# Asking for the first two experts' lists, weights and rows before the attention stage has ended

## The chip, the cores and the metric

The kernel runs on one core of a Trainium2 chip. The metric is the device time of one execution in microseconds (us): all input loads, the whole computation and the stores of the result.

## The reference, cut to what matters

One decoder layer over 64 sequences of 128 tokens, 256 wide: a linear-recurrence mixer, cross attention, and a mixture of experts, each with a residual and a layer norm. The change lies where the second turns into the third.

```python
x = _layernorm(x + mixer(x))
x = _layernorm(x + cross_attention(x, ctx))       # these rows are called x2 below
# mixture of experts: 32 experts, 4 of them for each token, at most 1280 tokens for one expert
shared = silu(xf @ sg) * (xf @ su) @ sd
top_scores, top_idx = top_k(masked_scores, 4)
buf[e_s, p_s] = xf[tok]                            # rows gathered by expert
h = silu(buf @ wg) * (buf @ wu)                    # per expert, 256 -> 512
out_e = h @ wd                                     # per expert, 512 -> 256
x = _layernorm(x + shared + routed)
```

## The kernel before, in words

Four stages follow one another, each a block of five instruction streams (SP, PE, ACT, DVE, POOL) with a barrier of all engines between two blocks: mixer, attention, experts, combination. All DMAs but the indirect ones are issued by SP, the indirect ones by POOL.

**Attention.** 16 groups of 4 sequences. All rows stand in one buffer `x` of 16 slots (`rows(k.x, g)`, 4 KB in each partition per group), which is released when the stage ends. As each group is done, SP stores its rows to `x_rows` in HBM, and POOL scatters, with 16 indirect DMAs a group, a list entry (token, destination, gate) for each token and chosen expert into `slot_token`. After the last group comes a tail: the routing of the last two groups, DVE's list of work items (`plan.count_items`, `plan.list_items`), and between them on PE, ACT and DVE the shared expert for the first three groups (`shared_turn`, `shared_up`, `shared_down`, `shared_sum`). SP's tail is `store(NG - 1)`, `store_shared(0)`, `plan.deliver` (the item list goes through HBM into `k.plan`, where engines can read it into registers), `store_shared(1)` and `(2)`, and the waits for all that was stored. POOL's tail ends with the last scatter.

**Experts.** An item is 256 list slots of one expert; there are 92 in this run. For each, SP reads the item's expert and first slot into registers and loads the list piece (`e_tok`, 3 KB), and gate, up and down weights (`e_raw_g`, `e_raw_u`, `e_raw_d`, 512 KB each); POOL gathers the rows (`e_xg`, two indirect DMAs of 128 rows); PE transposes them; ACT and DVE split weights and rows into a high and a low part; PE runs gate, up and down products out of three matmuls per chunk; POOL scatters the result. All of this is double-buffered. The first two items are unrolled: SP's `first` (L1777) issues list, gate and up of item 0, the same of item 1, both down loads, and two loads of x2 rows for the combination. ACT's `first` splits the four weight pieces of item 0 before it takes the transposed rows, and DVE follows it:

```python
                def first():
                    for m in range(HC):
                        weights_high(0, 0, 0, m)
                    turned(0)
                    item(0, 0, 0)
```

PE starts with `turn(0, 0, 0)`, which waits for the gathered rows, and `up(0, 0)`, which waits for the low parts of rows and weights. Each engine adds 1 or 16 to its semaphores on entry (`begin`) and reads the number of items into a register (`items_of`).

**Combination.** It adds shared rows, x2 rows and the four expert outputs of each token in a ring of four buffers (`acc`, `res`, `part`), and runs the shared expert for the other 13 groups.

## Time and profile before

| what | us |
|---|---|
| median of 3 runs | 2105.52 |
| lowest and highest | 2104.67, 2109.74 |
| span of the profiled execution | 2166.1 |
| attention stage ends, expert stage starts, in the profiled execution | between 1014.8 and 1020.6 |

The profile is one execution of its own, 60.6 us longer than the median; no other time of it is given than its span. Positions below are microseconds from the start of that span. PE is the matmul engine, PEld its weight loads, SPq the queue of DMAs that SP issues. In a timeline row the first number is the start, the second the time until the last of the merged instructions is done, and the brackets say how long the engine sat idle before and what ended it.

### The profile page before, as it was taken

Reading aid. Unit: us, or ns where it says so; the run is one execution under the profiler, and the core shown is the slowest. Engines: PE = TensorE matmul, PEld = TensorE weight load, DVE = VectorE, ACT = ScalarE, POOL = GpSimd, SP = SyncE. Lnnn points to the kernel's source line nnn. Section 1 sums busy time; section 2 is a strip of 40 time slices with the busy share of each in tenths; the row PEclk is TensorE's granted clock in tenths of the full one; section 3 lists DMA queues with packets and bytes.
Section 4 is the critical chain, followed back from the end, with each engine's and each line's share of the span. In section 5 each row is a group of like instructions: output and inputs, shape, how many; then the busy total and the mean of one; then the engine's idle time right before and its main releaser. Section 6 shows DMA issues by size and latency. Waiting matters only on the chain. (4 is left out here: it accounts for less than half of the span.)

```text
span 2166.1 us, 51696 instructions
## 1 busy us (share of the span) xinstructions
PE 2001.3 (92%) x14320; PEld 1794.5 (83%) x14320; DVE 1521.7 (70%) x3647; ACT 1254.7 (58%) x3478; POOL 1493.7 (69%) x1695
## 2 busy tenths in 40 slices
PE   8999799999999999875899999999999999579998
PEld 6888587777777777664899999999999999558887
DVE  7888467777776777662677777888888888335554
ACT  4556465655664556531677777777777777324443
POOL 5565315766665666663688888888888888458765
PEclk9999899999999999987899999999999999789999
DMA  4300132242233222401677766776777677356542
GB/s 140 88 0 1 43 127 79 85 151 78 78 105 113 94 78 93 131 20 53 230 229 235 232 234 226 230 240 229 236 235 236 232 238 233 122 216 237 203 165 98
DMA packets 244909, 329.95 MB, mean 152 GB/s; under 512 B 50074, under 2 KB 167234, under 8 KB 244836
## 3 DMA queue, kind: packets, MB, share of 16 engines
q1 hardware_dynamic: 218788, 279.97, 40.0%
q0 software_dynamic: 26048, 49.10, 6.2%
q8 instruction: 35, 0.57, 0.1%
q14 instruction: 38, 0.31, 0.0%
HBM read 236.17 MB, written 77.18 MB: 145 GB/s over the span
## 5 line engine op out<-in xcount | busy, mean ns | idle before, releaser
L1345 POOL DMA_INDIRECT slot_token<-a_entry,a_slot_i x256 | 261.8, 1022 | 158.2 <-issue 70.3
L1827 POOL DMA_INDIRECT part_rows<-e_out,e_dest x184 | 228.3, 1241 | 71.0 <-issue 56.6
L1819 POOL DMA_INDIRECT e_xg<-x_rows,e_tok x188 | 207.0, 1101 | 93.9 <-issue 56.2
L1960 ACT ACTIVATE e_sg<-e_g 128x256 f32<-128x256 f32 x368 | 141.8, 385 | 196.0 <-PE e_g L1652 186.5
L2009 DVE TENSOR_TENSOR e_h<-e_sg,e_u 128x256 f32<-128x256 f32 x368 | 157.3, 428 | 65.4 <-PE e_u L1652 28.2
L1170 ACT ACTIVATE a_prob<-a_s,a_ntop 128x128 f32<-128x128 f32 x512 | 180.9, 402 | 4.9 <-DVE a_ntop L1524 4.9
L2024 DVE TENSOR_SCALAR e_out<-e_d,e_dest 128x256 f32<-128x256 f32 x184 | 80.6, 480 | 139.6 <-PE e_d L1652 138.8
L1835 POOL TENSOR_TENSOR e_wd1l<-e_raw_d,e_wd1h 128x256 fp32r<-128x256 f32 x184 | 145.4, 827 | 5.7 <-ACT e_wd1h L1940 4.8
L1835 POOL TENSOR_TENSOR e_wd0l<-e_raw_d,e_wd0h 128x256 fp32r<-128x256 f32 x184 | 145.9, 829 | 4.8 <-ACT e_wd0h L1940 3.8
L1032 PE MATMUL a_o<-a_wo,a_ot 128*128 128x256 f32 x512 | 125.2, 389 | 8.4 <-DVE a_ot L1591 8.3
L1652 PE MATMUL e_d<-e_wd1h,e_ht1h 128*128 128x256 f32 x368 | 108.5, 295 | 24.5 <-issue 24.5
L1524 DVE TENSOR_REDUCE a_ntop<-a_s 128x4 f32<-128x512 f32 x128 | 82.4, 686 | 64.5 <-remote 41.6
L1170 ACT ACTIVATION_READ_ACCUMULATOR a_prob<-a_s,a_ntop 128x1 f32 x512 | 124.1, 242 | 0.0
L1032 PEld LDWEIGHTS a_o<-a_wo,a_ot 128*128 128x128 f32 x512 | 95.0, 196 | 20.0 <-DVE a_ot L1591 9.2
L2267 ACT ACTIVATE f_sg<-f_g 128x512 f32<-128x512 f32 x52 | 31.1, 599 | 134.4 <-PE f_g L1652 134.4
L1652 PE MATMUL e_g<-e_xth,e_wg1h 128*128 128x256 f32 x368 | 104.3, 284 | 3.9 <-DVE e_xtl L1995 3.7
L1652 PE MATMUL e_d<-e_wd0h,e_ht0h 128*128 128x256 f32 x368 | 107.6, 292 | 0.0
L1652 PE MATMUL e_g<-e_xth,e_wg0h 128*128 128x256 f32 x368 | 105.1, 286 | 1.4 <-DVE e_xtl L1995 1.4
L1652 PE MATMUL e_d<-e_wd1h,e_ht1l 128*128 128x256 f32 x368 | 104.5, 284 | 0.0
L1652 PE MATMUL e_d<-e_wd1l,e_ht1h 128*128 128x256 f32 x368 | 104.5, 284 | 0.0
L1652 PE MATMUL e_g<-e_xtl,e_wg0h 128*128 128x256 f32 x368 | 104.2, 283 | 0.0
L1652 PE MATMUL e_u<-e_xth,e_wu0l 128*128 128x256 f32 x368 | 104.2, 283 | 0.0
(397 smaller groups left out, 7604.8 us busy)
## 6 DMA issues: line engine op xcount, KB each, us to landing
e_raw_g<-in_eg SPq DMA_DIRECT2D x94, 512.0 KB
e_raw_u<-in_eu SPq DMA_DIRECT2D x94, 512.0 KB
e_raw_d<-in_ed SPq DMA_DIRECT2D x93, 512.0 KB
part_rows<-a_zero SPq DMA_DIRECT2D x16, 2048.0 KB
f_part<-part_rows SPq DMA_DIRECT2D x16, 2048.0 KB, 9.5
x<-in_x SPq DMA_DIRECT2D x16, 512.0 KB, 4.0
x_rows<-x SPq DMA_DIRECT2D x16, 512.0 KB
out_rows<-f_res SPq DMA_DIRECT2D x16, 512.0 KB, 10.1
```

Of the source, the lines that this page charges most:

```text
L1032: last = pe.matmul(bank_o[:, 0:D], ot[:, m, :], wo[:, m, :], start=(m == 0), stop=(m == IC - 1))
L1170: last = act.activation(prob[b % 2][:, h, :], bank_s[r][:, m * T:(m + 1) * T], ACT.Exp, bias=ntop[b % 2][:, h:h + 1], accum_out=den[b % 2] ...
L1345: pool.indirect_dma_start(k.slot_tok, bass.IndirectOffsetOnAxis(ap=slot_i[:, j, q:q + 1], axis=0), entry[:, j, q, :], None, bounds_check=S ...
L1524: last = dve.tensor_reduce(ntop[b % 2][:, r * IC:(r + 1) * IC], bank_s[r][:].rearrange("p (m t) -> p m t", m=IC), AX.X, ALU.max, negate=True)
L1652: last = pe.matmul(out, a, b, start=(n == 0 and t == 0), stop=(n == len(chunks) - 1 and t == 2))
L1819: pool.indirect_dma_start(xg[a][:, n, :], None, k.x2_d, bass.IndirectOffsetOnAxis(ap=tok[a][:, n, 0:1], axis=0))\
L1827: pool.indirect_dma_start(k.part_d, bass.IndirectOffsetOnAxis(ap=dest[a][:, n, 1:2], axis=0), out[a][:, n, :], None).then_inc(put[a], 16)
L1835: pool.tensor_tensor(wd[par][1][:, m, :], raw_d[par][:, m, :], wd[par][0][:, m, :].bitcast(F32), ALU.subtract).then_inc(dl_rdy, 1)
L1960: act.activation(sg[m % 2][:], bank_g[m % 2][:, 0:SETW], ACT.Silu).then_inc(sg_rdy, 1)
L2009: dve.tensor_tensor(hid[m % 2], sg[m % 2][:], bank_u[m % 2][:, 0:SETW], ALU.mult)\
L2024: dve.tensor_scalar(out[a][:, n, :], bank_d[0:RT, (n % 2) * D:(n % 2 + 1) * D], gate[:, n, 2:3], None, ALU.mult).then_inc(out_rdy, 1)
L2267: act.activation(sg[m % 2][:], bank_g[m % 2][:], ACT.Silu).then_inc(sg_rdy, 1)
```

## The change

Gate, up and down weights, list pieces and gathered rows of items 0 and 1 are asked for inside the attention stage. Their SBUF buffers are no longer allocated by the expert stage: they become views of slots 3 to 9 of `x`, which is now kept for the whole kernel, and whose slots 3 to 9 hold rows that have been stored to HBM. The combination's `acc`, `res` and `part` (16 slots in all) become views of `x` as well. Two list buffers and ten semaphores are made for the whole kernel. The zero fill of `x_rows`' spare rows gets a semaphore of its own (`spare_in`), so that POOL can wait for it.

```diff
                 store(NG - 1)
                 store_shared(0)
                 plan.deliver(sp)
+                sp.wait_ge(x2_out, DMA + 16 * NG)
+                for w in range(2):
+                    e = expert_of(sp, k, w)
+                    sp.dma_start(k.raw_g[w], one_expert(k.gate_d, e)).then_inc(k.g_in[w], 16)
+                    sp.dma_start(k.raw_u[w], one_expert(k.up_d, e)).then_inc(k.u_in[w], 16)
+                    start = slots_of(sp, k, w)
+                    if w == 0:
+                        sp.wait_ge(scattered, 16 * TG * K * NG)
+                        apart(sp, k.past_sp)
+                    sp.dma_start(k.tok[w][:], k.slot_tok[bass.ds(start, SETW), :].rearrange("(p n) a -> p n a", n=TI))\
+                        .then_inc(k.tok_in[w], 16)
+                for w in range(2):
+                    e = expert_of(sp, k, w)
+                    sp.dma_start(k.raw_d[w], one_expert(k.down_d, e)).then_inc(k.d_in[w], 16)
                 for n in range(1, SG):
                     store_shared(n)
-                sp.wait_ge(x2_out, DMA + 16 * NG)
-                sp.wait_ge(filled, DMA + 16 * (NG + 1 + SG))
+                sp.wait_ge(spare_in, 16)
+                sp.wait_ge(filled, DMA + 16 * (NG + SG))
                 sp.wait_ge(blanked, DMA + 32)
...
                 scatter(NG - 1, range(TG), False)
+                pool.wait_ge(x2_out, DMA + 16 * NG)
+                pool.wait_ge(spare_in, 16)
+                for w in range(2):
+                    pool.wait_ge(k.tok_in[w], 16)
+                    apart(pool, k.past_pool)
+                    gather_rows(pool, k, w)
...
                 def first():
-                    for w in range(2):
-                        load_tok(w, w)
-                        load_gate(w, w)
-                        load_up(w, w)
-                    for w in range(2):
-                        load_down(w, w)
                     for i in range(2):
                         first_rows = k.x2_d[(SG + i) * GW:(SG + i + 1) * GW, :]
...
                 def first():
-                    gather(0, 0, 0)
-                    gather(1, 1, 0)
                     item(0, 0, 0)
                     item(1, 1, 0)
...
-        acc, res = ([p.sb(f"{n}{i}", [P, TG, D]) for i in range(RING)] for n in ("acc", "res"))
-        part = [p.sb(f"part{i}", [P, TG, K, D]) for i in range(2)]
+        acc, res = ([grouped(in_rows(k, n * RING + i)) for i in range(RING)] for n in range(2))
+        part = [k.x[:, (2 * RING + K * i) * GX:(2 * RING + K * (i + 1)) * GX]
+                .rearrange("p (t q d) -> p t q d", t=TG, q=K) for i in range(2)]
...
+def in_rows(k, g):
+    return k.x[:, g * GX:(g + 1) * GX]
...
+def first_tiles(k, sem):
+    def wide(g):
+        return in_rows(k, g).rearrange("p (c n) -> p c n", c=DC)
+    k.raw_g, k.raw_u = [wide(SG + i) for i in range(2)], [wide(SG + 2 + i) for i in range(2)]
+    k.raw_d = [in_rows(k, SG + 4 + i).rearrange("p (c n) -> p c n", c=HC) for i in range(2)]
+    k.xg = [in_rows(k, SG + 6)[:, i * TI * D:(i + 1) * TI * D].rearrange("p (n d) -> p n d", n=TI) for i in range(2)]
...
+def gather_rows(pool, k, a):
+    for n in range(TI):
+        pool.indirect_dma_start(k.xg[a][:, n, :], None, k.x2_d,
+                                bass.IndirectOffsetOnAxis(ap=k.tok[a][:, n, 0:1], axis=0)).then_inc(k.rows_in[a], 16)
```

`expert_of` and `slots_of` read the expert and the first slot of an item from `k.plan` into a register, as the expert stage did.

## Rows read from the trace of the kernel before

**Rows 1.** The page's head: span and number of instructions.
```profile
span 2166.1 us, 51696 instructions
```

**Rows 2.** Windows: stretch, its us, busy us of each engine, granted clock, DMA.
```profile
core 0: us, PE busy (x) PEld busy (x) DVE busy (x) ACT busy (x) POOL busy (x), PEclk, DMA share, GB/s
...
996.00:1000.00 4.00, 3.34 (x8) 2.70 (x9) 1.98 (x3) 2.10 (x4) 0.54 (x2) 0.50 0.01 2
1000.00:1004.00 4.00, 4.00 (x18) 2.97 (x16) 1.29 (x2) 1.86 (x4) 0.00 (x0) 0.97 0.01 2
...
1030.00:1036.00 6.00, 4.59 (x21) 4.19 (x20) 1.65 (x3) 1.50 (x3) 1.05 (x2) 0.50 1.06 355
1036.00:1039.00 3.00, 3.00 (x20) 3.00 (x20) 1.42 (x4) 1.75 (x5) 0.00 (x0) 0.70 1.09 361
1200.00:1800.00 600.00, 600.00 (x5071) 599.92 (x5070) 481.28 (x1000) 435.99 (x1133) 524.83 (x533) 1.00 0.71 232
```

**Rows 3.** Timeline of all engines, from the tail's last PE work to expert work.
```profile
1013.43 0.28 PE L1652 MATMUL a_o<-wd_both,a_htl 128*128 128x256 f32 x1
...
1023.07 1.07 POOL L1819 DMA_INDIRECT e_xg<-x_rows,e_tok  x1 [25.86 <-DMA e_tok<-slot_token]
...
1025.07 1.15 ACT L1933 ACTIVATE e_wg0h<-e_raw_g 128x512 fp32r<-128x512 f32 x2 [19.57 <-DMA e_raw_g<-in_eg]
...
1027.90 1.15 ACT L1933 ACTIVATE e_wu0h<-e_raw_u 128x512 fp32r<-128x512 f32 x2 [1.68 <-DMA e_raw_u<-in_eu]
1028.56 1.29 DVE L1989 TENSOR_TENSOR e_wu0l<-e_raw_u,e_wu0h 128x512 fp32r<-128x512 f32 x2 [1.53 <-ACT e_wu0h L1933]
1028.88 1.21 POOL L1819 DMA_INDIRECT e_xg<-x_rows,e_tok  x1 [3.47 <-DMA e_tok<-slot_token]
...
1029.47 1.12 PE L1873 MATMUL e_t<-ident,e_xg 128*128 128x128 f32 x4 [15.76 <-DMA e_xg<-x_rows,e_tok]
...
1030.62 0.60 ACT L1946 ACTIVATE e_xth<-e_t 128x512 fp32r<-128x512 f32 x1 [1.57 <-PE e_t L1873]
...
1031.25 0.69 DVE L1995 TENSOR_TENSOR e_xtl<-e_t,e_xth 128x512 fp32r<-128x512 f32 x1 [1.40 <-ACT e_xth L1946]
...
1032.00 0.58 PE L1652 MATMUL e_g<-e_xth,e_wg0h 128*128 128x256 f32 x1 [1.41 <-DVE e_xtl L1995]
```

**Rows 4.** Timeline of SP's DMA queue, 980 to 1040 us (21.59 spans both stores).
```profile
984.11 0.25 SPq L724 DMA_DIRECT2D plan<-item_list  x1
993.26 21.59 SPq L933 DMA_DIRECT2D shared_rows<-x  x2
1020.60 0.36 SPq L1739 DMA_DIRECT2D e_tok<-slot_token  x1
1021.72 0.38 SPq L1746 DMA_DIRECT2D e_raw_g<-in_eg  x1
...
1024.00 0.35 SPq L1739 DMA_DIRECT2D e_tok<-slot_token  x1
```

**Rows 5.** Waits of SP's queue, 980 to 1030 us: total us, times, longest.
```profile
SPq L947 <- DMA shared_rows<-x: 2.5, 1, 2.5
```

**Rows 6.** Timelines at the two other changes of stage: engine starts.
```profile
236.15 2.06 ACT L369 ACTIVATE x<-x,m_off,m_rs 128x256 f32<-128x256 f32 x4
...
239.60 1.94 PE L963 MATMUL a_a<-ident,x 128*128 128x128 f32 x8 [3.98 <-issue]
...
1905.47 0.38 SPq L2114 DMA_DIRECT2D xs<-shared_rows  x1
```

**Rows 7.** Timeline of PE at the start of the combination stage.
```profile
1905.83 1.94 PE L2197 MATMUL f_t<-ident,xs 128*128 128x128 f32 x8 [10.55 <-DVEq L72]
```

**Rows 8.** Timeline of the attention tail, 990 to 1000 us, three engines.
```profile
992.48 0.69 DVE L1571 TENSOR_TENSOR x<-a_o,x 128x512 f32<-128x512 f32 x1 [9.87 <-remote]
...
996.01 1.08 ACT L1224 ACTIVATE v<-a_s 128x512 f32<-128x512 f32 x2 [19.61 <-remote]
996.61 0.60 POOL L1353 TENSOR_SCALAR a_entry<-a_entry 128x16 int32<-128x16 int32 x2 [2.83 <-DMA slot_token<-a_entry,a_slot_i]
```

**Rows 9.** Timeline of PE near the end of the expert stage.
```profile
1890.28 0.57 PE L1652 MATMUL e_d<-e_wd1h,e_ht1h 128*128 128x256 f32 x1 [24.53 <-issue]
```

More of the change, by code:

```diff
@@ L900, in _ @@
                 sp.wait_ge(zero_rdy, 1)
-                sp.dma_start(k.x2_d[B * T:B * T + SETW, :].rearrange("(p n) d -> p n d", n=TI), spare).then_inc(filled, 16)
+                sp.dma_start(k.x2_d[B * T:B * T + SETW, :].rearrange("(p n) d -> p n d", n=TI), spare).then_inc(spare_in, 16)
                 def store(g):
@@ L1662, in expert_stage @@
         p = Parts(nc, ctx, "e_")
[L1663 to L1664 removed]
+        raw_g, raw_u, raw_d, tok, xg = k.raw_g, k.raw_u, k.raw_d, k.tok, k.xg
         wg = [[p.sb(f"wg{i}{h}", [P, DC, HID], F32R) for h in "hl"] for i in range(2)]
         wu = [[p.sb(f"wu{i}{h}", [P, DC, HID], F32R) for h in "hl"] for i in range(2)]
[L1667 removed]
         wd = [[p.sb(f"wd{i}{h}", [P, HC, D], F32R) for h in "hl"] for i in range(2)]
[L1669 removed]
         dest = [p.sb(f"dest{i}", [RT, TI, 3], I32) for i in range(2)]
[L1671 removed]
         xt = [p.sb(f"xt{h}", [P, DC, SETW], F32R) for h in "hl"]
@@ L1680, in expert_stage @@
         hid = [bank[:, 0:SETW] for bank in bank_h]
-        g_in, u_in, d_in, tok_in, x_in, dest_in = ([p.sem(f"{n}{i}") for i in range(2)]
-                                                   for n in ("g_in", "u_in", "d_in", "tok_in", "x_in", "dest_in"))
+        g_in, u_in, d_in, tok_in, x_in = k.g_in, k.u_in, k.d_in, k.tok_in, k.rows_in
+        dest_in = [p.sem(f"dest_in{i}") for i in range(2)]
         put = [p.sem(f"put{i}") for i in range(2)]
@@ L1723, in _ @@
                 begin(sp, dma=(*g_in, *u_in, *d_in, *tok_in, *dest_in, *k.xs_in[:2]))
-                def one(d, e):
-                    return d[:, bass.ds(e, 1), :, :].rearrange("p a c n -> p (a c) n")
-                def expert(w):
-                    return sp.value_load(k.plan[0:1, bass.ds(w * 4 + 1, 1)], min_val=0, max_val=E - 1)
-                def slots(w):
-                    return sp.value_load(k.plan[0:1, bass.ds(w * 4, 1)], min_val=0, max_val=SLOTS)
                 def load_tok(w, a):
-                    start = slots(w)
+                    start = slots_of(sp, k, w)
                     if at_least(w, 2):
@@ L1817, in gather @@
                     apart(pool, k.past_pool)
-                    for n in range(TI):
-                        pool.indirect_dma_start(xg[a][:, n, :], None, k.x2_d,
-                                                bass.IndirectOffsetOnAxis(ap=tok[a][:, n, 0:1], axis=0))\
-                            .then_inc(x_in[a], 16)
+                    gather_rows(pool, k, a)
                 def put_rows(w, a):
@@ L2349, with one_expert, expert_of, slots_of @@
     pass
+def in_rows(k, g):
[6 more added lines that the diff above has]
+    k.xg = [in_rows(k, SG + 6)[:, i * TI * D:(i + 1) * TI * D].rearrange("p (n d) -> p n d", n=TI) for i in range(2)]
+    k.g_in, k.u_in, k.d_in, k.tok_in, k.rows_in = ([sem(f"{n}{i}") for i in range(2)]
+                                                   for n in ("g_in", "u_in", "d_in", "tok_in", "rows_in"))
+    k.gate_d = k.weights["eg"].rearrange("e (c p) n -> p e c n", p=P)
+    k.up_d = k.weights["eu"].rearrange("e (c p) n -> p e c n", p=P)
+    k.down_d = k.weights["ed"].rearrange("e (c p) n -> p e c n", p=P)
+def one_expert(weights, e):
+    return weights[:, bass.ds(e, 1), :, :].rearrange("p a c n -> p (a c) n")
+def expert_of(sp, k, w):
+    return sp.value_load(k.plan[0:1, bass.ds(w * 4 + 1, 1)], min_val=0, max_val=E - 1)
+def slots_of(sp, k, w):
+    return sp.value_load(k.plan[0:1, bass.ds(w * 4, 1)], min_val=0, max_val=SLOTS)
+def gather_rows(pool, k, a):
+    for n in range(TI):
+        pool.indirect_dma_start(k.xg[a][:, n, :], None, k.x2_d,
+                                bass.IndirectOffsetOnAxis(ap=k.tok[a][:, n, 0:1], axis=0)).then_inc(k.rows_in[a], 16)
 def build(nc, dram):
@@ L2374, in build @@
         k.shared_d = nc.dram_tensor("shared_rows", [SG * GW, D], F32).ap()
+        k.tok = [sb(f"tok{i}", [RT, TI, 3], I32) for i in range(2)]
+        k.x, k.weights = sb("x", [P, B * D]), dram
+        first_tiles(k, lambda name: ctx.enter_context(nc.semaphore(name)))
         with ExitStack() as early:
```

25 lines of the change are left out of this document (8 added, 17 removed).

## The prediction

> **What bounds the kernel now.** I read the page's head first: the profiled execution spans 2166.1 us [rows 1], 60.6 us more than the median of the runs. Part of that excess is visible as pauses in which an engine waits for nothing the kernel asks for (24.53 us on PE in one item [rows 9], 9.87 us on DVE in the attention tail [rows 8]). So I make the sum of the change on the profiled positions, and say separately what such a pause covers.
>
> Then the windows. In the long middle of the expert stage PE is busy for 600.00 of 600 us at full clock, with the DMA engines at a share of 0.71 [rows 2]. So this stage is bound by PE: a microsecond saved before PE's first product moves every item, and the combination behind them, forward by the same. A microsecond saved on loads alone, once PE runs, is worth nothing.
>
> Then the timeline between the stages, which is where the change acts. The reader should follow the chain by hand. PE's last matmul of the attention tail starts at 1013.43 [rows 3]; DVE adds it, SP issues the last shared-row store, whose issue ends at 993.26 + 21.59 = 1014.85 [rows 4], and then waits 2.5 us for its landing [rows 5], so the stage is over at about 1017.4. SP's first load of the expert stage comes at 1020.60 [rows 4]. ACT starts at 1025.07, when the first gate weights are there, and again at 1027.90 for the up weights; PE's transposes start at 1029.47, when the gathered rows are there; the first product starts at 1032.00 [rows 3]. Between 1013.7 and 1032.0 PE does four transposes. Its long wait, 15.76 us, ends on the gather; the gather in its turn waited for the list [rows 3]. This is what the change addresses: list 2.47 us from issue to use (1020.60 to 1023.07), gather 6.4 us from POOL's start to PE's.
>
> **The change part by part.** *The start of the expert stage.* With lists, weights and rows on the chip, ACT, DVE and PE start as soon as the barrier lets them. Call ACT's first instruction S. For S the trace has three indications. SP's first issue at 1020.60 [rows 4] follows two register reads (number of items, first slot), where ACT has only one; two SP loads with one read each lie 1.12 us apart, of which 0.36 is the issue, so a read is about 0.75 us, and S = 1020.60 - 0.75 = 1019.9. As the early bound I take the first change of stage: ACT's last work ends at 236.15 + 2.06 = 238.21 and PE starts at 239.60, 1.4 us later [rows 6], which gives 1017.4 + 1.4 = 1018.8. As the late bound, in the combination stage, whose first rows are already on the chip, PE starts 0.36 us after SP's first issue (1905.83 against 1905.47) [rows 6, 7], which gives 1021.0. I take 1019.9.
>
> From S the chain is ACT's four pieces, 1.15 us for each two, so the second pair starts at S + 1.1; DVE ends the second pair 1.95 us after that pair began (1028.56 + 1.29 - 1027.90), at S + 3.05; meanwhile PE has transposed (1.12) and ACT has split the rows (0.60); DVE takes the rows' low part after the weights', and PE's first product starts 0.75 us behind its beginning (1032.00 - 1031.25): S + 3.8 [rows 3]. With S = 1019.9 that is 1023.7 instead of 1032.0: **8.3 us less**, and 9.4 to 7.2 by the two bounds. Nothing behind it eats this: from here on item 0 needs the down weights, item 1 its weights and rows, all of them on the chip. Item 2's loads wait for what DVE and PE have done with item 0, so they move forward with it.
>
> *The clock.* Before, PE ran at 0.50 of its clock up to 1036 and at 0.70 on average from 1036 to 1039 [rows 2], so the first product saw about 6.6 us of the lower level (1.2 GHz), after an idle stretch of 15.8 us. After the shorter pause in the tail [rows 8] PE was busy for 3.34 us at 0.50 from 996 to 1000, and the stretch from 1000 to 1004 has 0.97 [rows 2]: 3 to 4 us. The new idle stretch, 6 us to the transposes and 10 to the products, lies between. If the low level ends as early as after the short gap, half of the 3 us difference is won, 1.5 us; if nothing changes, none. I take **0.5 us less**.
>
> *SP's queue in the tail.* SP moves eight loads behind the delivery of the plan, and in front of two shared-row stores. The plan is asked for at 984.11 [rows 4], so gate and up of item 0 go out near 987. Then SP waits for all scatters, which POOL sees landed at 996.61 [rows 8]. That is the new wait: behind it stand list 0, gate 1, up 1, list 1, down 0, down 1 and both shared-row stores. With 0.4 us for each issue and 0.75 for each of four reads, some 5.5 us, SP is through at about 1002.2. The store of group 1 was issued at 993.26 before [rows 4], but nobody waits for it before the stage ends. The store of group 2 is ready only at about 1014.5, 0.36 us before its issue ends at 1014.85, and is issued then, as before. The four weights behind the wait are 2.1 MB; at 355 GB/s [rows 2] that is 5.9 us, and they have landed by 1006. So on the profiled positions the cost is zero, covered by PE, ACT and DVE's work on the shared expert, with some 8 us to spare.
>
> That cover contains the 9.87 us pause. If the timed runs do not have it, the last store is ready at 1004.6. It then stands behind the rest of the weights (to 1006) and the group 1 store (0.52 MB, 1.5 us), and four gathers (0.52 MB, 1.5 us) mix in: it lands up to 4.4 us later. If they do have it, nothing. I take **1.5 us more**, and 0 and 4.4 as ends.
>
> The row to weigh here is DMA share and rate in this part of the tail: 0.01 and 2 GB/s from 996 to 1004 [rows 2], so there is room for the loads. The Trainium skill (DMA: Bandwidth & Descriptors, "Issuing engines are not separate DMA queues") says that transfers started by SP and by POOL run on the same 16 engines and interleave. By that rule weights, scatters and stores share one rate, which is the 4.4 us end; by queues of their own the gathers' 1.5 us would fall away.
>
> *POOL.* It moves four gathers ahead of the barrier and gains waits for rows, spare rows and lists; nothing is queued behind them in this stage but the barrier. List 0 is there 2.5 us after its issue near 997, and two gathers take 2.6 us. List 1 took 4.9 us behind two weight loads (1024.00 to 1028.88) [rows 3, 4] and is asked for near 999.5, so the last gather is issued by 1007. The barrier opens at 1017.4, or 1007.5 without the pause: cost zero either way, but then by only half a microsecond.
>
> *Memory.* The views are of the same shape and use the same instructions, and the x2 rows of slots 3 to 9 were stored long before; no instruction is added in the expert or combination stage. Cost zero.
>
> **The sum.** -8.3 - 0.5 + 1.5 = -7.3 us. On the profiled positions, with the pause, it is -8.8: span 2157.3. The items behind are bound by PE in both, so I carry -7.3 over to the median: 2105.5 - 7.3 = **2098.2 us**.
>
> **Rivals.** *A, the gain is partly given back:* either the tail's store lands at the late end (4.4) or another wait takes the place of the loads, such as ACT, DVE or PE starting 2 to 4 us after S because three streams enter code that they used to enter under cover of the loads. For it speaks that all of them sat idle until 1025 or later, so the trace shows nothing of what they could have done earlier; against it, the starts at the other changes of stage, 1.4 us and 0.36 us [rows 6, 7]. With both bounds, 7.2 - 4.4 = 2.8 us of gain: 2102.7.
>
> *B, the clock and the barrier go well:* S by its early bound, 1.5 us from the clock, no loss in the tail: 9.4 + 1.5 = 10.9 us, 2094.6.
>
> *C, slower:* SP's wait for the scatters holds the last store. Weights of item 0 now run while the last few scatters are issued. If each scatter, 12-byte entries in 128 pieces, had to stand behind such loads, the wait at 996.61 would end later by d, and SP is through at 1002.2 + d. It decides from d = 12.3 us on the profiled positions, or 2.4 us without the pause; beyond that each microsecond is paid in full. The change is slower than before from 8.8 us beyond that point on, and by over 0.3% from 15.1 us beyond it, 17.5 us in all. 1 MB of weights at 355 GB/s lasts 3 us, which speaks strongly against it. At 17.5 us: 2112.
>
> *D, it does nothing:* something else sets PE's first product, for instance the rows of item 0 landing after the barrier anyway. They are asked for 16 us before 1017.4, or 6 us without the pause, and took 6.4 us at worst in the trace. Time: 2105.5.
>
> **How the numbers follow.** Measurement of this kernel can tell about 0.3%, 6.3 us: faster means below 2099.2. Forecast (gain 6.3 to 9.5): 0.50. B: 0.12. A: 0.28. D: 0.05. C and its kind: 0.05. So faster 0.62, same 0.33, slower 0.05. The range reaches from B, 2094.6, to past A, 2104.0; it leaves out D, C and the far end of B.
>
> **What would show it.** In the profile after: e_raw_g, e_raw_u, e_raw_d and e_tok of two items in SP's queue between 987 and 1003, with a hole up to the scatters' landing; POOL's four gathers before 1008; ACT's first split within 1 us of 1019.9, counted as 2.5 us behind the landing of the last store; the first product 3.8 us later; PE's share of 1.00 from the third item on. The prediction is wrong if ACT starts more than 2 us after that, if the last store's landing moves away from DVE's last sum, or if PE's work on the first items grows new waits for loads.

## The result, and the profile after

| kernel | median of the runs, us | lowest and highest | ratio to before, 95% interval |
|---|---|---|---|
| before | 2105.1 | 2104.17, 2109.74 | |
| changed | 2094.2 | 2092.2, 2095.48 | 0.9943 [0.9928, 0.9957] |
| changed, a second series on another chip | 2096.8 | 2095.08, 2098.51 | 0.9960 [0.9947, 0.9972] |

Faster, as forecast, but by 10.9 us in the first series where 7.3 were forecast: 0.4 us beyond the fast end of the range. The second series gives 8.3 us. The spans are 1.7 to 1.8 us below the times of the same executions.

The profiled execution shown ahead of the prediction was 60.6 us too long. The kernel before was therefore profiled once more (e1 below: time 2108.6, span 2106.8), and the comparisons here are with that trace.

The changed kernel's timeline at the change of stage, all engines; the brackets give the idle time before the instruction and what ended it. They answer to [rows 3, 4]:

```profile
939.76 0.41 SPq L946 DMA_DIRECT2D x<-in_eg  x1
940.27 0.41 SPq L947 DMA_DIRECT2D x<-in_eu  x1
947.64 0.36 SPq L952 DMA_DIRECT2D tok<-slot_token  x1
...
950.28 1.07 POOL L2380 DMA_INDIRECT x<-x_rows,tok  x1 [2.12 <-DMA tok<-slot_token]
...
951.93 1.55 SPq L956 DMA_DIRECT2D x<-in_ed  x2
953.52 4.54 SPq L933 DMA_DIRECT2D shared_rows<-x  x2
...
956.95 0.69 DVE L1591 TENSOR_TENSOR x<-a_o,x 128x512 f32<-128x512 f32 x1 [2.11 <-PE a_o L1672]
957.05 0.96 POOL L2380 DMA_INDIRECT x<-x_rows,tok  x1 [4.43 <-DMA tok<-slot_token]
958.31 0.96 POOL L2380 DMA_INDIRECT x<-x_rows,tok  x1 [0.30 <-issue]
965.74 1.15 ACT L1925 ACTIVATE e_wg0h<-x 128x512 fp32r<-128x512 f32 x2 [17.01 <-issue]
...
966.16 1.11 PE L1865 MATMUL e_t<-ident,x 128*128 128x128 f32 x4 [9.24 <-issue]
...
969.55 0.58 PE L1672 MATMUL e_g<-e_xth,e_wg0h 128*128 128x256 f32 x1 [2.29 <-DVE e_xtl L1987]
```

And SP's waits in the same execution (line, what it waited for, total us, times, longest), which answer to [rows 5]:

```profile
SPq L62 <- DMA slot_token<-a_entry,a_slot_i: 6.1, 1, 6.1
SPq L961 <- DMA shared_rows<-x: 4.6, 1, 4.6
```

The same place in the kernel before (e1), one row for each link of its chain:

```profile
958.60 0.69 DVE L1571 TENSOR_TENSOR x<-a_o,x 128x512 f32<-128x512 f32 x1 [2.06 <-PE a_o L1652]
959.32 0.37 SPq L933 DMA_DIRECT2D shared_rows<-x  x1
965.43 0.36 SPq L1739 DMA_DIRECT2D e_tok<-slot_token  x1
...
969.83 1.15 ACT L1933 ACTIVATE e_wg0h<-e_raw_g 128x512 fp32r<-128x512 f32 x2 [19.36 <-DMA e_raw_g<-in_eg]
...
974.52 1.11 PE L1873 MATMUL e_t<-ident,e_xg 128*128 128x128 f32 x4 [15.96 <-DMA e_xg<-x_rows,e_tok]
...
977.04 0.58 PE L1652 MATMUL e_g<-e_xth,e_wg0h 128*128 128x256 f32 x1 [1.41 <-DVE e_xtl L1995]
```

From DVE's last sum of the attention to PE's first product it was 977.04 - 958.60 = 18.4 us and is 969.55 - 956.95 = 12.6 us: **5.8 us** won at the head. PE's transposes no longer end their wait on the gather; the bracket says "issue", which here covers the barrier between the stages. That is the change doing what it says. Two things went against it. The last store takes 4.6 us to land, where it took 2.5 [rows 5]. And the barrier waits for POOL. At the end of the attention block (L877) each engine's queue of instructions ends with a DRAIN, and the barrier's first event comes when the last DRAIN has ended. The changed kernel's, and behind them those of e7, whose gathers are back in the expert stage (count, then ns, then the start in us):

```profile
L877 POOLq EVENT_SEMAPHORE  x2: 17/17/17, 964.4 to 964.5; - x2
...
L877 POOLq DRAIN  x1: 7047/7047/7047, 957.3 to 957.3; - x1
...
L877 SPq DRAIN  x1: 13/13/13, 962.9 to 962.9; - x1
```

```profile
L877 POOLq EVENT_SEMAPHORE  x2: 17/17/17, 961.7 to 961.7; - x2
L877 POOLq DRAIN  x1: 4097/4097/4097, 947.4 to 947.4; - x1
...
L877 SPq DRAIN  x1: 13/13/13, 961.6 to 961.6; - x1
```

In the changed kernel SP is done at 962.9, and POOL's DRAIN ends only at 957.3 + 7.05 = 964.4: the barrier opens 1.5 us later than the last store asks for. By the packets of the trace the last gathered rows land at 962.57, 1.8 us before that DRAIN ends. In e7, with no gathers in the tail, POOL has long been done when SP comes. So the barrier, too, opens later than before: 3.9 us behind DVE's last sum in e1, 7.5 us here. Of these 3.6 us more, 2.1 are the store and 1.5 the gathers. From the barrier to the first product it was 14.5 us and is 5.1. The difference of the two is the 5.8 us.

From the first product to the first transposes of the combination (PE `f_t`) it was 1846.77 - 977.04 = 869.7 us and is 1834.52 - 969.55 = 865.0: **4.8 us** more, inside a stage of which the prediction said that only the clock would change, by 0.5. The other 3.1 us between the two spans (2106.8 and 2093.1) lie ahead of DVE's last sum (1.6) and behind `f_t` (1.5); the same two stretches differ by as much between executions of kernels with the same memory, so nothing is read from them. The windows show where the 4.8 us come from. PE's busy time, its count of matmuls (x), and the granted clock (PEclk); first e1:

```profile
core 0: us, PE busy (x) PEld busy (x) DVE busy (x) ACT busy (x) POOL busy (x), PEclk, DMA share, GB/s
1000.00:1200.00 200.00, 200.00 (x1694) 200.00 (x1693) 154.36 (x334) 145.24 (x380) 150.05 (x178) 1.00 0.70 233
1500.00:1700.00 200.00, 200.00 (x1694) 199.99 (x1693) 163.44 (x334) 145.04 (x379) 175.46 (x179) 1.00 0.72 235
```

and the changed kernel:

```profile
1000.00:1200.00 200.00, 200.00 (x1732) 200.00 (x1731) 157.25 (x343) 149.22 (x389) 174.70 (x182) 1.00 0.72 239
1500.00:1700.00 200.00, 199.14 (x1689) 197.05 (x1688) 168.31 (x333) 145.15 (x378) 175.68 (x178) 1.00 0.71 232
```

In the first window PE is busy for 200.00 of 200 us at a clock of 1.00 in both, and yet does 1732 matmuls instead of 1694. "100% busy" had hidden a rate. In the second the gain is gone: 1689, PE has 0.86 us of idle time, and PEld 2.95. Item by item (from one group of transposes to the next) the changed kernel takes 8.78 us on average from the third item to the 31st, near 1240 us, and 9.02 after it; the kernel before takes 8.98 and 8.99. Counted from the first product, the changed kernel leads by 0.5 us at the second item, by 6.0 at the 34th, and by 4.3 at the start of the last: the faster items give about 5.5 us and the slower ones take 1.7 back. So some 4 us net come from the rate of the items and 0.5 from the clock.

### The profile page after: what moved, and what is told of

It reads as the page before. It is cut to its first block and busy times, and to the rows that moved or that the text cites. A ratio compares the mean times of both kernels' runs of the same rounds, so it can differ in the third digit from the quotient of the medians.

```text
span 2093.1 us, 51690 instructions
## 1 busy us (share of the span) xinstructions
PE 1973.9 (94%) x14320; PEld 1772.8 (85%) x14320; DVE 1533.5 (73%) x3647; ACT 1255.7 (60%) x3478; POOL 1488.2 (71%) x1695
## 5 line engine op out<-in xcount | busy, mean ns | idle before, releaser
L2380 POOL DMA_INDIRECT x<-x_rows,tok x188 | 206.8, 1100 | 75.9 <-issue 56.1
L1829 POOL TENSOR_TENSOR e_wd1l<-x,e_wd1h 128x256 fp32r<-128x256 f32 x184 | 145.5, 828 | 5.7 <-ACT e_wd1h L1932 4.8
L1829 POOL TENSOR_TENSOR e_wd0l<-x,e_wd0h 128x256 fp32r<-128x256 f32 x184 | 145.5, 829 | 5.4 <-ACT e_wd0h L1932 4.4
L1672 PE MATMUL e_d<-e_wd1h,e_ht1h 128*128 128x256 f32 x368 | 107.0, 291 | 24.5 <-issue 24.5
L1046 PEld LDWEIGHTS a_o<-a_wo,a_ot 128*128 128x128 f32 x512 | 93.8, 193 | 19.2 <-DVE a_ot L1611 8.8
L1672 PE MATMUL e_g<-e_xth,e_wg0l 128*128 128x256 f32 x368 | 103.1, 280 | 0.0
## 6 DMA issues: line engine op xcount, KB each, us to landing
out_rows<-x SPq DMA_DIRECT2D x16, 512.0 KB, 10.3
```

Of the source, the lines that this page charges most:

```text
L1046: last = pe.matmul(bank_o[:, 0:D], ot[:, m, :], wo[:, m, :], start=(m == 0), stop=(m == IC - 1))
L1672: last = pe.matmul(out, a, b, start=(n == 0 and t == 0), stop=(n == len(chunks) - 1 and t == 2))
L1829: pool.tensor_tensor(wd[par][1][:, m, :], raw_d[par][:, m, :], wd[par][0][:, m, :].bitcast(F32), ALU.subtract).then_inc(dl_rdy, 1)
L2380: pool.indirect_dma_start(k.xg[a][:, n, :], None, k.x2_d, bass.IndirectOffsetOnAxis(ap=k.tok[a][:, n, 0:1], axis=0)).then_inc(k.rows_in[a] ...
```

## The experiments

Each kernel was timed against the kernel before on the same chip. The attention's tail alone, from DVE's sum near 841 us to its last, differs between executions of all these kernels from 111 to 116 us, old ones and new ones alike, a spread as wide as that of the medians; so the lengths inside a trace carry the argument, and the medians confirm it. Several medians lie 1 to 5 us below the time expected (e4, e5, e11, e16, e17), and those of e2 and e3 2 us above it. The changed kernel was not timed beside e2 to e4; its own ratio to the kernel before, 0.9943 or 0.9960 (e8), is what theirs are held against.

The head differs between executions as well, by the tail. This table has every kernel with loads in the tail, and e1 (us; all but the landing counted from DVE's last sum, the first column back from it):

| kernel | down loads all issued, before the last sum | last store lands in | SP comes to the barrier | barrier opens | first product |
|---|---|---|---|---|---|
| changed | 3.5 | 4.6 | 5.9 | 7.5 | 12.6 |
| e8, the same | 3.7 | 4.3 | 5.7 | 7.2 | 12.3 |
| e3 | 1.2 | 6.3 | 7.7 | 8.7 | 13.9 |
| e6 | 1.1 | 6.5 | 7.8 | 8.8 | 13.9 |
| e2 | -0.1 | 8.1 | 9.6 | 10.6 | 15.8 |
| e7, no gathers in the tail | 1.3 | 5.3 | 6.7 | 6.7 | 16.9 |
| e4, no down loads in the tail | | 3.1 | 4.5 | 6.5 | 11.6 |
| e12, the same | | 2.6 | 3.9 | 6.4 | 11.6 |
| e1 | | 2.5 | 3.9 | 3.9 | 18.4 |

The closer the down loads come to the last store, the longer it takes to land; without them it takes 2.6 to 3.1 us. With gathers in the tail the barrier opens 1.0 to 2.5 us behind SP, and in every kernel without them 0.02 to 0.03 us behind it. From the barrier to the first product all seven kernels with early loads and gathers take 5.13 us. So the 5.8 us of the head are those of one execution: with the same loads in the tail the others give 6.1 (e8), 4.6 (e3), 4.5 (e6) and 2.7 (e2).

**e1, the kernel before again** (no edit).

> The kernel before, profiled once more, to have a trace without the pauses that made its first one 60 us longer. Theory POOL (the expert stage is paced by POOL's instructions, not by PE's): from the third item on POOL runs without idle time but for the fixed gaps between its indirect DMAs, items come every 8.9 to 9.0 us, and the change gained where POOL's unbroken chain starts earlier, by about 9 to 12 us counted from DVE's last sum of the attention stage. Theory PE (the one of the prediction): the start of PE's first product moved by the whole gain, so counted from DVE's last sum the first product comes some 11 us later here than in the changed kernel, not 5.6 us as the two traces at hand say.

2108.55 us in its one execution. The trace is the one used above. Neither theory came out as written: the first product came 5.8 us later than in the changed kernel and not 11, and in the first window POOL is busy for 150 of 200 us and waits for ACT. The idle stretch of 9.87 us in the tail [rows 8] is not in it. The 24.5 us before the last `e_d` group [rows 9] are, in both kernels, whose spans are free of any excess:

```profile
1831.65 0.58 PE L1652 MATMUL e_d<-e_wd1h,e_ht1h 128*128 128x256 f32 x1 [24.53 <-issue]
```

So this row was read wrongly: it is a fixed part of the stage's end (24.5 or 24.6 us in every kernel here), presumably PE's way through the rounds of the loop that have no items, and no part of the 60.6 us. Those lie in the attention stage, which from PE's first instruction to DVE's last sum took 774.2 us in the first profile and 715.2 in this one.

**e2, 5 us more work for POOL**, once, behind items 0 and 1 of the changed kernel:

```diff
+                    for n in range(2):
+                        pool.tensor_tensor(in_rows(k, 13 + n), in_rows(k, 11), in_rows(k, 12), ALU.add)
```

> The changed kernel with two additions of 128 x 1024 elements on POOL, into unused slots of x, right after its work for item 1: 4.8 us more on POOL, by the 2.40 us of the same shape in the combination stage. Nothing waits for them but POOL itself. Theory POOL: 4 to 5 us slower than the changed kernel, 2098 to 2099, because POOL has no idle time behind that point. Theory PE: within 1 us of the changed kernel, because POOL has slack in every item.

2101.0 us, ratio 0.9978 [0.9966, 0.9990]. The addition took 5.21 us, and the stage from first product to `f_t` was 869.9 us long instead of 865.0: nearly all of it was paid, within the first ten items. POOL has no slack over the stage of the changed kernel. The time is 2 us above what was expected; the late landing of this execution (8.1 us, in the table) has nothing to do with the edit, which stands behind the barrier.

**e3, POOL's four subtractions of an item in one instruction** (changed kernel; the two waits on them adapted):

```diff
-                    for m in range(HC):
-                        pool.wait_ge(dh_rdy, ONE + HC * w + m + 1)
-                        pool.tensor_tensor(wd[par][1][:, m, :], raw_d[par][:, m, :], wd[par][0][:, m, :].bitcast(F32),
-                                           ALU.subtract).then_inc(dl_rdy, 1)
+                    pool.wait_ge(dh_rdy, ONE + HC * (w + 1))
+                    pool.tensor_tensor(wd[par][1][:], raw_d[par], wd[par][0][:].bitcast(F32),
+                                       ALU.subtract).then_inc(dl_rdy, 1)
```

> The changed kernel with POOL's four subtractions of 128 x 256 per item (2.81 us) made as one of 128 x 1024 (2.40 us). Same result. Theory POOL: an item gets 0.4 us shorter until PE's own 8.62 us bind, so 15 to 30 us less in all, 2064 to 2079. Theory PE: no change, or up to 2 us slower, since PE's down product can start only when all four parts are done.

2081.4 us, ratio 0.9888 [0.9868, 0.9908]. The windows of e3:

```profile
1000.00:1200.00 200.00, 200.00 (x1733) 200.00 (x1732) 163.24 (x343) 149.24 (x389) 157.27 (x116) 1.00 0.73 241
1500.00:1700.00 200.00, 200.00 (x1736) 200.00 (x1736) 164.27 (x343) 149.74 (x390) 157.28 (x115) 1.00 0.73 239
```

Now the rate of the first window lasts: 8.78 us an item to the end. POOL's groups from 1500 to 1700 us, the changed kernel first (busy us, mean ns | idle before, and what ended it), show what the edit relieved:

```profile
L1821 POOL DMA_INDIRECT part_rows<-e_out,e_dest x44 | 53.3, 1211 | 10.4 <-issue 10.0 <-DMA tok<-slot_token 0.3
...
L1829 POOL TENSOR_TENSOR e_wd0l<-x,e_wd0h 128x256 fp32r<-128x256 f32 x46 | 38.7, 876 | 0.3
```

```profile
L1828 POOL TENSOR_TENSOR e_wd1l<-x,e_wd1h 128x1024 fp32r<-128x1024 f32 x12 | 28.9, 2407 | 9.4 <-ACT e_wd1h L1931 9.4
```

Four subtractions of 876 ns are 3.50 us; the one takes 2.41. In the changed kernel POOL is idle for 0.3 and 0.2 us in all ahead of its two groups of subtractions in that stretch; in e3 it waits 0.8 us an item for ACT. The gain is less than the 15 to 30 us expected, because 8.62 us is only the shorter of two kinds of item: they come at 8.62 or about 8.90, and PE's own average is 8.78. The stage is 850.8 us long, 14.2 less than in the changed kernel.

**e4, the two loads of down weights left in the expert stage** (changed kernel):

```diff
-                for w in range(2):
-                    e = expert_of(sp, k, w)
-                    sp.dma_start(k.raw_d[w], one_expert(k.down_d, e)).then_inc(k.d_in[w], 16)
                 for n in range(1, SG):
                     store_shared(n)
...
                 def first():
+                    load_down(0, 0)
+                    load_down(1, 1)
```

> The changed kernel with the two down loads left at the start of the expert stage (1 MB less in the attention tail). It prices the contention in the tail: in the changed kernel the last shared-row store took 4.6 us to land, against 2.5 us before. Both theories: the landing comes back to 2.5 to 3 us. If the down weights are not missed later, the kernel gains 1 to 2 us (2092 to 2093); if their arrival near 971 delays the list load for item 2 and with it POOL, it gains nothing or loses up to 2 us.

2089.4 us, ratio 0.9922 [0.9905, 0.9939], on a chip on which the changed kernel itself was not timed. In the trace the last store lands in 3.1 us instead of 4.6, and from last sum to first product it is 11.6 us instead of 12.6, the stage behind it 865.8: 1 us, not 5. SP comes to the barrier 1.5 us earlier, but POOL's DRAIN now holds it for 2.0 us more. e12 below does not show the 5 us either.

The kernels from here on, but for e7, e8, e11 and e12, ask where the faster matmuls come from.

**e5, the changed kernel's memory with the old order of loads:** lists, weights and gathers of both items are asked for in the expert stage again, in the tiles of the changed kernel.

> This kernel has the changed kernel's tiles in the changed kernel's places, but the first two items' lists, weights and rows are all asked for in the expert stage again, as before. Theory L (TensorE's matmul spacing depends on where the tiles lie): within the expert stage the 48 gate and up products of an item take 5.4 to 5.6 us instead of 5.70, so the time from the first transposes of the expert stage to the first ones of the last stage is 2 to 4 us shorter than the 872.25 us of the kernel before (868.36 in the changed one), and the time is about 2101 to 2103. Theory O (the spacing changed with the order, that is with how the engines' work falls against one another after an earlier start): 5.70 us and 872 us as before, the time 2105, a ratio of 1.000. Theory B (the page of the kernel before had only an unlucky execution): no difference in spacing between any of the kernels beyond what repeats differ by.

2099.6 us, ratio 0.9969 [0.9958, 0.9979]. From last sum to first product 19.2 us (18.2 to 19.0 in the kernels with the old memory); from there to `f_t` 866.0 us, as in the changed kernel, and 1729 matmuls in the first window. So the 4 us of the stage come with the memory, and not with the earlier start.

**e6, the two lists 64 bytes wide instead of 24** (changed kernel):

```diff
-        k.tok = [sb(f"tok{i}", [RT, TI, 3], I32) for i in range(2)]
+        k.tok = [sb(f"tok{i}", [RT, TI, 8], I32)[:, :, 0:3] for i in range(2)]
```

> The changed kernel with each of the two lists in 64 bytes per partition instead of 24, so that all later tiles lie 80 bytes further on; nothing else. Theory L in its narrow form (the offset of the tiles within a block of memory decides): the item pitch differs from the changed kernel's, to 8.98 us throughout with 5.70 us for gate and up (time about 2097 to 2098), or faster throughout. If the offset is of no account: as the changed kernel, 2093 to 2096, gate and up 5.44 to 5.6 us.

2097.4 us, 0.9961 [0.9948, 0.9974]; the stage 863.8 us. Items of 8.75 and 9.00 us: still the faster rate. So moving all later tiles on by 80 bytes does not bring the old one back.

**e7, only the gathers back in the expert stage** (changed kernel).

> The changed kernel with only the four indirect gathers of the first two items moved back to the expert stage; lists and weights are still asked for in the attention's tail. The prediction's own sum: the gathers cannot begin before the barrier is passed, so GpSimd's two gathers of the first item and the landing of their rows are on the path again: the first transposes move from the last sum + 9.2 us to about + 13 to 14 us, the time is 4 to 5 us above the changed kernel's, 2098 to 2100. Rival (the gathers were not what held the start, the weights' landing was): within 1.5 us of the changed kernel.

2099.1 us, 0.9968 [0.9956, 0.9981]. From last sum to first product 16.9 us: 4.3 to 4.5 us over the changed kernel's 12.6 and 12.3, as expected. That is a difference of two effects. From the barrier to the first product it is 10.2 us instead of 5.1, and the barrier opens 0.5 to 0.8 us earlier, because no gathers hold it. The medians differ by 2.3 (e8).

**e8, the changed kernel again,** beside e5 to e7.

> The changed kernel again, on the chip that runs the three beside it: 2093 to 2096; gate and up of an item 5.44 us in some items and 5.6 on average. Theory B (the spacing differs from execution to execution) expects another pattern: 5.70 throughout, or 5.44 throughout.

2096.8 us, 0.9960 [0.9947, 0.9972]. 12.3 us at the head and 865.4 in the stage: the pattern repeats.

**e9 and e10, the old tiles in another order or higher.** e9 allocates raw weights and gathered rows behind all other tiles; e10 puts 36 KB of nothing ahead of all:

```diff
+        p.sb("pad", [P, 36 * 256])
         raw_g = [p.sb(f"raw_g{i}", [P, DC, HID]) for i in range(2)]
```

> The kernel before with one difference: the tiles that the transfers of the expert stage fill (the raw gate, up and down weights and the gathered rows) are allocated behind all other tiles of that stage instead of ahead of and between them, so that the tiles TensorE reads lie 16 to 24 KB further down. Theory S (what counts is that the tiles which transfers and the other engines read are apart from those TensorE reads, as the stored rows' memory is in the changed kernel): matmul spacing of the changed kernel, 0.113 to 0.118 us, items of 8.62 and 8.90 us, the expert stage 3.5 to 4 us shorter, time 2101. Theory P (the place of TensorE's own tiles counts, high in memory in the changed kernel): no gain, as the kernel before, 8.98 us an item, 2105.

> The kernel before with an unused tile of 36 KB per partition ahead of the tiles of the expert stage: all of them lie 36 KB higher, in the same order. Theory P: spacing and items as in the changed kernel (8.62 and 8.90 us), time about 2101. Theory S: as the kernel before, 8.98 us an item, 2105. If both kernels of this pair show the changed kernel's spacing, neither S nor P but only some particular conflict of the old places is left; if neither does, the place of the tiles is not shown to be the cause.

2106.7 us, 1.0004 [0.9996, 1.0013], and 2105.3, 0.9996 [0.9987, 1.0005]. Items of 8.98 and 9.00 us. Neither brings the faster rate, so both theories as they stood fall: height alone does not do it, nor does taking the raw tiles away from between the others. But e10's height did something: its stage is 872.8 us long against e1's 869.7, and its down products start 0.1236 us apart on average instead of 0.1222.

**e11, e3's edit on the kernel before.**

> The kernel before with GpSimd's four subtractions of an item as one, the edit that made the changed kernel 13 us faster. Theory: in the kernel before TensorE sets the item at 8.98 us by its own spacing, and GpSimd only follows; relieving it gives nothing: 2104 to 2106, items 8.98 us. Rival (GpSimd set the item in both kernels): faster by 8 to 13 us here too, items 8.6 to 8.9 us.

2102.6 us, 0.9990 [0.9981, 0.9999]. Items of 8.98 us, and the windows of e11 have the old count:

```profile
1000.00:1200.00 200.00, 200.00 (x1694) 200.00 (x1693) 155.54 (x336) 145.51 (x380) 158.58 (x113) 1.00 0.71 233
1500.00:1700.00 200.00, 200.00 (x1694) 200.00 (x1693) 155.10 (x334) 144.82 (x377) 159.03 (x112) 1.00 0.71 232
```

The same edit is worth 13 us in the changed kernel and 2.5, at the limit of what can be told, in the old one, whose stage stays at 869.7 us. There PE's own rate sets the item; in the changed kernel it is POOL from about item 31 on. The old kernel was close to it: in e1's second window POOL is busy for 175.46 us and idle for 24.8, all but 0.4 of them the gaps marked "issue" ahead of its indirect instructions.

**e12, both edits,** e3's and e4's, on the changed kernel.

> The changed kernel with both edits that made it faster: GpSimd's four subtractions of an item as one, and the two loads of the down weights left in the expert stage. The first gives 13 us; of the second, 1.5 us are the landing of the tail's last store (4.6 to 3.1 us), which is all it can give if its measured 5 us were mostly scatter of runs: 2079 to 2081; if the 5 us are real and add up: 2075 to 2077.

2080.3 us, 0.9889 [0.9875, 0.9904]: e3's gain and no more by the medians, so most of e4's 5 us was scatter; a microsecond or two either way can't be told by them. Head 11.6 us, stage 851.6. It beats both kernels, the old one by 24 to 25 us.

**e13 to e15, semaphores or tiles.** e13: only the ten semaphores of the first loads are taken early, in the kernel before. e14: e5 with these semaphores back in their old place. e15: e5 with the gathered rows in tiles of their own.

> The kernel before with one difference: the ten semaphores of the first loads (weights, lists, gathered rows) are taken at the program's start, as in the changed kernel, so that all semaphores taken after them have other numbers; every tile stays where it was. Theory M (the place of the loaded tiles in the kept memory makes TensorE's spacing shorter and GpSimd's indirect transfers longer): nothing, 2105, items 8.98 us, matmuls 282 ns in the mean, an indirect instruction 0.97 to 1.00 us. Theory N (it is the numbers of the semaphores or another difference of the programs): 278 ns, items 8.62 to 8.92, indirect instructions 1.16 to 1.25 us, time 2101.

> The kernel with the changed kernel's memory and the old order of loads, with the ten semaphores back among those of the expert stage: the tiles alone are changed. Theory M: as the kernel with the changed memory and both (ratio 0.997, items 8.62 to 8.92 us, matmul 278 ns, indirect 1.16 to 1.25 us). Theory N: as the kernel before, 8.98 us and 2105.

> The kernel with the changed kernel's memory and the old order of loads, with only the two tiles of gathered rows in memory of their own again, between the down weights and the transposed rows as before. If the place of the gathered rows, which TensorE reads in its transposes and the indirect transfers fill, is what counts: items of 8.98 us, indirect instructions of 0.97 to 1.00 us. If it is the raw weights' place: 8.62 to 8.92 us and 1.16 to 1.25 us, ratio 0.997.

| | ratio, 95% interval | stage, us |
|---|---|---|
| e13 | 1.0001 [0.9987, 1.0015] | 870.1 |
| e14 | 0.9973 [0.9957, 0.9989] | 867.0 |
| e15 | 0.9987 [0.9975, 0.9998] | 867.0 |

By items (8.79 in e14 and 8.80 in e15 up to the 26th, 8.98 in e13) the tiles do it, without the semaphores and without the gathered rows. e15's median alone would hardly tell it from the kernel before. POOL's longer indirect instructions, which the expectations tied to the memory, are not tied to it: e11, with the old memory, has 1.20 and 1.17 us for them too.

**e16 to e18, which tiles.** e16: the kernel before, with raw weights, rows and lists ahead of all tiles that PE reads. e17: the same with 36 KB between them. e18: e5 with the raw weights and the gathered rows 12 KB lower.

```diff
         raw_u = [p.sb(f"raw_u{i}", [P, DC, HID]) for i in range(2)]
+        raw_d = [p.sb(f"raw_d{i}", [P, HC, D]) for i in range(2)]
+        xg = [p.sb(f"xg{i}", [RT, TI, D]) for i in range(2)]
+        tok = [p.sb(f"tok{i}", [RT, TI, 3], I32) for i in range(2)]
+        p.sb("pad", [P, 36 * 256])     # e17 only
         wg = [[p.sb(f"wg{i}{h}", [P, DC, HID], F32R) for h in "hl"] for i in range(2)]
```

> The kernel before with the tiles that transfers fill (raw weights, gathered rows, lists) all ahead of the tiles TensorE reads, no pad: TensorE's weight tiles lie 12 KB higher than before and next to one another, as in the changed kernel, but 36 KB lower than there. Theory T (TensorE's tiles next to one another without a raw tile between them, the raw ones below them): items of 8.62 to 8.92 us, 2101. Theory P2 (their absolute place, as with the 36 KB): as before, 8.98 us, 2105. Theory R (the place of the raw weights in the stored rows' memory): as before, 2105.

> The same with an unused tile of 36 KB between the raw tiles and those that TensorE reads: every tile that TensorE reads in its products then has exactly the changed kernel's place, while the raw tiles lie 24 KB lower than there. Theories T and P2: items of 8.62 to 8.92 us, 2101. Theory R: 8.98 us, 2105.

> The kernel with the changed kernel's memory and the old order of loads, with the raw weights and gathered rows 12 KB lower within the stored rows' memory; everything else in its place. Theories T and P2: as that kernel, ratio 0.997, items of 8.62 to 8.92 us. Theory R in its narrow form (a particular distance of 12 KB matters): another spacing.

2099.6 us, 0.9974 [0.9962, 0.9987]; 2095.5, 0.9949 [0.9932, 0.9965]; 2100.8, 0.9976 [0.9966, 0.9985]. Stage 862.0, 866.0 and 866.4 us. All three have the faster rate, 8.77 to 8.79 us an item up to the 26th. e16 is the kernel before with three lines moved up. Its groups of products from 1000 to 1240 us, behind those of e9, which has the same tiles in yet another order; e9 first, then e16:

```profile
L1652 PE MATMUL e_g<-e_xtl,e_wg1h 128*128 128x256 f32 x105 | 29.6, 282 | 0.0
...
L1652 PE MATMUL e_d<-e_wd1h,e_ht1l 128*128 128x256 f32 x112 | 31.5, 281 | 0.0
```

```profile
L1652 PE MATMUL e_g<-e_xtl,e_wg1h 128*128 128x256 f32 x112 | 31.1, 278 | 0.0
...
L1652 PE MATMUL e_d<-e_wd1h,e_ht1l 128*128 128x256 f32 x112 | 31.1, 277 | 0.0
```

The single matmul is listed with 281 to 282 ns in most groups of the one and 277 to 278 in most of the other, and all groups of `e_g`, `e_u` and `e_d` went down, but for `e_g<-e_xth,e_wg0h`, which has 282 in both. The spacing of their starts tells the same: in items of 8.98 us the 48 gate and up products take 5.70 us and the 24 down products 2.93; in the kernels with the faster rate 5.44 or 5.70, by the item, and in most items 2.83.

The attention's tail shows the same of other products. The shared expert's products of 512 columns start 0.227 us apart in every kernel that has `x` in its old place (e1, e9 to e11, e13, e16, e17) and 0.233, in e6 0.232, in all those with `x` in the new one. There the changed memory is the slower one, by 0.3 us over the last two groups.

**What stays open.** Shown: with the same instructions, semaphores and order of loads, the place of the tiles in SBUF alone changes the matmuls' spacing (e14, e16, against e1, e13). Excluded as what decides: the gathered rows' place (e15), 12 KB in the raw weights' place (e18), 36 KB in height (e10 has no gain by it, e16 has the gain without it), 80 bytes in the place of all tiles from the weights on (e6). One thing separates all runs without an exception: in those with the faster rate (the changed kernel, e2 to e8, e12, e14 to e18) the two lists, 24 or 64 bytes per partition each, lie ahead of the weight tiles that PE reads; in the others (before, e1, e9, e10, e11, e13) they lie behind them. Of the other tiles only the two `e_dest`, behind the weights in every kernel, are not a multiple of 1 KB, so the lists' place sets the offset between the weights and the transposed rows, which go into the same products; it sets the weights' own offset within a KB as well, and the runs do not part the two. But no kernel moved the lists alone, so this is what the runs agree with, and not a cause that was shown. A kernel that does only that would settle it; it wasn't tried.

## Why the prediction was right or wrong

**The chain at the start: right, and sized too low.** It said that ACT, DVE and PE start from the barrier and that the first product follows ACT's first split by 3.8 us; it was 969.55 - 965.74 = 3.8. ACT's first split came 1.3 us behind the opening of the barrier, which is the early bound (1.4 us) and not the 1019.9 that was taken. By that bound the chain gives 9.4 us, and it gave 9.4: 14.5 us from barrier to first product in e1, 5.1 in the changed kernel.

**The tail: sized too low, and one wait in it missed.** The term was 1.5 us, with 4.4 as its end; the barrier opened 3.6 us later (3.9 to 7.5 behind the last sum), and 6.7 in e2. One of the prediction's own signs of being wrong, the last store's landing moving away from DVE's last sum, was there. Of the 3.6 us, 2.1 are the store behind the weights, the mechanism that the prediction named. The other 1.5 are the gathers: "The barrier opens at 1017.4, or 1007.5 without the pause: cost zero either way" counted when the last gather is issued, and the barrier waits for POOL's DRAIN, which ends 1.8 us behind the rows' landing. List 1 held that gather until 958.31. So the head gave 9.4 - 3.6 = 5.8 us where 8.3 - 1.5 = 6.8 were expected, two misses that partly cancel; that the total is so near is luck.

The rule weighed in the tail (the Trainium skill, DMA: Bandwidth & Descriptors, "Issuing engines are not separate DMA queues") has transfers started by SP and by POOL share the same DMA engines. e4 does not test it, since SP starts both the down loads and the store. e7 does, against e3, whose down loads come as close to the last store: with POOL's gathers in the tail the store took 6.3 us, without them 5.3. That agrees with the rule, by one execution of each.

**The clock: right in size, partly by luck.** The lower level (0.50, 1.2 GHz) ran from the first product to about 973.2 in the changed kernel and to 981.7 in e1, 3.65 against 4.64 us, worked out from the windows that hold the step (0.60 over 970 to 974, 0.54 over 978 to 982). Half of the difference is 0.5 us. But by the spacing of the products that stretch is 3.2 to 5.9 us long in the kernels with early loads and 4.0 to 5.7 in the others, so one pair does not show 0.5 us to be the gain. And the 6.6 us of the prediction is a slip: 0.70 on average over 1036 to 1039 [rows 2] puts the step at 1037.8, 5.8 us behind the first product.

**The step that failed** is "Memory. ... Cost zero". The tiles moved, and with them the matmuls' spacing: about 4 of the 4.8 us in the stage. With it the sum is -9.4 (chain) + 3.6 (tail) - 0.5 (clock) - 4.0 = -10.3, against 10.9 and 8.3 measured. Which offset of the tiles does it stays open. That the stage is "bound by PE" because PE is busy for 600 of 600 us [rows 2] was true of the kernel before (e11) but did not say at what rate. POOL, to which the prediction gave no cost, was near its limit already; once PE had become faster it took over as the bound, and kept 13 us from showing (e3).

**The rivals.** B gave the right time, 2094.6, and its early bound of S was right; but it had no loss in the tail, where 3.6 us were lost, and 1.5 us from the clock instead of 0.5; the 4 us of the tiles, which it did not have, made up for both. A's late landing did occur, at half its price here and above its price in e2 (5.6 us). C's hold was seen in small: SP waited 6.1 us for the scatters, issued list 0 at 947.64 and was through its loads at 953.5, 4 us before the last store was ready; in e2 it was through only 0.6 us before. D is refuted by the 5.8 us.

## What to carry to other kernels

A move of a tile is an edit of its own: when a change shifts where the operands of back-to-back matmuls lie, compare matmuls per microsecond in a long window, not the busy share, before crediting the rest of the change. And ask what an engine at 88% of a window would do if the bound moved by 2%: here POOL (175 of 200 us busy, the rest the gaps ahead of its indirect instructions, 0.3 us for most) became the bound after some 30 items, and merging four short instructions into one was worth more than the change studied. And a transfer that is asked for early is not free because nobody reads it yet: if it is still under way at the end of a block, the barrier waits for it. Leaving only the second item's gathers in the expert stage was not tried.

## What was not expected of the hardware

- The same matmuls (128x128 weights, 256 columns) at a granted clock of 1.00 take 2.93 or 2.83 us for the 24 of the down weights, by the tiles' places, and 5.70 or 5.44 us for the 48 of gate and up, in the kernels with the faster rate by the item.
- The barrier at the end of a block opened 0.02 to 0.03 us behind SP in the 13 traces without gathers in flight, and 1.0 to 2.5 us behind it in the seven with them, each time 1.8 us after the last gathered rows had landed.
- POOL's subtraction of 128x256 took 736 ns on average early in e1 (1000 to 1240 us) and 867 ns in 1500 to 1700, its indirect store 998 and 1216 ns, with the same code. The step falls between the 26th and the 45th item in the old kernel as in the changed one; its cause was not looked for. One subtraction of 128x1024 took 2407 ns, less than four of the quickest (4 x 736 = 2944).
